# An early decay table, transposes in groups between output tiles, later splits of the output weights and six banks at the end, in a gated linear-attention kernel

## The reference

```
xn   = layernorm(x)
qkv  = silu(xn @ w_qkv.T); 16 heads of 128
for each block of 64 tokens and each head, with s the head's slope:
    out = (q * decay_q) @ kv + ((q @ k.T) * decay) @ v
    kv  = exp(-64 s) * kv + (k * decay_k).T @ v
out  = norm_w * out / rms(out) over all 16 heads
s    = (sigmoid(xn @ w_gate.T) * out) @ w_out.T
f    = xn * sum(top 8 weights) + top 8 weights @ expert_bias   (softmax router, 64 experts)
y    = x + s * silu(f)
```

## Time and profile before

| | |
|---|---|
| median of 3 runs | 1200.68 us (1197.55 to 1203.21) |
| profiled execution, its own time | 1200.99 us |
| its span, first to last instruction | 1199.2 us |
| mean granted clock of PE | 0.973 of full speed |
| PE busy | 1121.5 us (94%) |
| DVE busy | 843.1 us (70%) |
| ACT busy | 611.6 us (51%) |
| POOL busy | 128.2 us (11%) |
| DMA | 85.46 MB, 71 GB/s |

### The profile page before, as it was taken

The page is one execution under the profiler, slowest core; times in us unless marked ns, Lnnn a source line. Parts: engine busy times, 40 slices in busy tenths (PEclk is TensorE's granted clock), DMA queues, the critical chain, the costliest instruction groups (busy, mean ns, idle before and its releaser), DMA issues.

```text
span 1199.2 us, 16261 instructions
## 1 busy us (share of the span) xinstructions
PE 1121.5 (94%) x6366; PEld 968.0 (81%) x6366; DVE 843.1 (70%) x1613; ACT 611.6 (51%) x1308; POOL 128.2 (11%) x123
## 2 busy tenths in 40 slices
PE   6949999999999999999789899999999999999996
PEld 4747988889897888889668679898888888898884
DVE  7447678685777868786654877777668687766655
ACT  4436455464655555464524554655555474645542
POOL 4100000000000010202220000000000000000002
PEclk8979999999999999999889899999999999999998
DMA  3162112121111323322210611111212122111403
GB/s 126 36 192 63 41 53 71 54 78 55 53 41 48 97 71 91 112 62 80 78 55 19 219 64 52 62 51 49 78 50 74 36 71 65 50 54 45 132 1 123
DMA packets 37566, 85.46 MB, mean 71 GB/s; under 512 B 4320, under 2 KB 8688, under 8 KB 37488
## 3 DMA queue, kind: packets, MB, share of 16 engines
q1 hardware_dynamic: 37488, 84.41, 22.0%
HBM read 73.88 MB, written 14.71 MB: 74 GB/s over the span
## 4 chain that ended last, share of the span: by engine, by line
PE 64%; DVE 16%; ACT 13%; DMA 3%; SPq 1%; issue 1%; POOL 1%; DVEq 0%
PE psR L215 40%; PE psB L215 12%; PE psO L215 6%; PE psS L215 5%; ACT sg L513 3%; DVE gl L377 3%; ACT gh L376 2%; ACT zh L709 1%; DVE ql L372 1%; SPq L82 1%; DVE T L704 1%; DVE T L555 1%; DVE xl L298 1%; ACT woh L376 1%; DMA dtab<-dscr 1%
## 5 line engine op out<-in xcount | busy, mean ns | idle before, releaser
L724 POOL TENSOR_TENSOR ss<-ss,sq 128x512 f32<-128x512 f32 x58 | 78.4, 1352 | 840.9 <-ACT sq L710 840.9
L215 PE MATMUL psR<-xh,gh 128*128 128x512 f32 x384 | 130.7, 421 | 4.4 <-DVE gl L377 2.3
L215 PE MATMUL psR<-xl,gh 128*128 128x512 f32 x384 | 120.5, 395 | 0.0
L709 ACT ACTIVATE zh<-T,nw 128x512 fp32r<-128x512 f32 x64 | 46.3, 724 | 143.4 <-DVE T L704 143.4
L215 PE MATMUL psR<-xh,gl 128*128 128x512 f32 x384 | 119.3, 392 | 0.0
L215 PE MATMUL psR<-woh,zh 128*128 128x512 f32 x252 | 106.2, 422 | 1.9 <-DVE yacc L763 1.6
L215 PE MATMUL psB<-xh,gh 128*128 128x512 f32 x288 | 93.1, 404 | 15.0 <-ACT psB L506 8.4
L215 PE MATMUL psR<-woh,zl 128*128 128x512 f32 x252 | 100.1, 397 | 0.0
L215 PE MATMUL psR<-wol,zh 128*128 128x512 f32 x252 | 99.8, 396 | 0.0
L215 PE MATMUL psR<-wvh,xh 128*128 128x256 f32 x512 | 87.2, 293 | 8.4 <-DVE xl L298 5.8
L215 PE MATMUL psB<-xh,gl 128*128 128x512 f32 x288 | 89.7, 393 | 0.0
(11 more groups left out here) (186 smaller groups left out, 2668.9 us busy)
## 6 DMA issues: line engine op xcount, KB each, us to landing
raw<-w SPq DMA_DIRECT2D x80, 512.0 KB, 3.5
D<-dtab SPq DMA_DIRECT2D x32, 256.0 KB, 2.7
xs<-x SPq DMA_DIRECT2D x28, 256.0 KB, 3.2
gscr<-xs SPq DMA_DIRECT2D x16, 256.0 KB, 2.0
xs<-xnorm SPq DMA_DIRECT2D x16, 256.0 KB, 3.4
out_dram<-yacc SPq DMA_DIRECT2D x16, 256.0 KB, 2.2
dtab<-dscr SPq DMA_DIRECT2D x2, 1792.0 KB
xs<-gscr SPq DMA_DIRECT2D x14, 256.0 KB, 4.5
```

The source lines that it names most:

```text
L215: return lambda e: e.matmul(o, l, r, start=start, stop=stop, skip_group_check=shared)
L709: hi = act.do(lambda a: a.activation(zh[:, i, :], T[:, t, :], ACT.Copy, scale=half), z, nw_ev, *zfree)
L724: a = lane.do(lambda g: g.tensor_add(ss[:, j, :], ss[:, j, :], sq[:, :]), q, ss_ev.get(j))
```

## The change

- The power for `dval` is queued ahead of the value weights; its DMAs and the spreading come right behind the normalisations of tiles 4 to 7, before the key weights.
- `value_weights(0)` takes its third step ahead of `stat` of tiles 4 to 7. All four mingles at the start, and those at the change of phase, are on DVE.
- `tile_b` becomes a generator `groups_b`; `second_rows` yields after each group. `closing` alternates these groups with output tiles of pair 6 (`do_out(v - 1, 1)`, moved here from `heads`) and pair 7, with key weights and with the values of the next phase.
- In `opening`, `do_scores(v, 1)` comes earlier, and the value weights of the next pair are taken inside `second_keys`, where `do_state(v, 1)` comes behind p5.
- `gates` hands its output-weight split over to the next `first_keys`, behind p6 and p2.
- `fetch` and `finish_tile` are one tile per hook instead of two.
- In `gated`, `last` settles before the sum of squares. At the end, two tiles are seeded in two banks of `psS` before the others, and `add_out` of tiles 0 and 1 comes before the last mix.

```diff
         def groups_b(t, a, b, nb):
...
+            yield
@@ gated
             owed.append(rest)
+            if last:
+                settle()
@@ leave
-            else:
+            elif i >= 0:
                 ring.give(i, e)
@@ hooks of the second phase
-        for k in range(4):
-            for tt in (2 * k, 2 * k + 1):
-                later(8, k, lambda tt=tt: fetch(tt))
-                later(8, k + 1, lambda tt=tt: finish_tile(tt // 4, tt))
+        for tt in range(8):
+            later(*step((8, 0), tt), lambda tt=tt: fetch(tt))
+            later(*step((8, 0), tt + 1), lambda tt=tt: finish_tile(tt // 4, tt))
@@ start
+        e = pool.do(lambda g: g.tensor_scalar(dexp[:, :], dexp[:, :], sl[:, :], None, ALU.mult), sl_ev, dexp_ev)
+        dval_ev = pool.do(lambda g: g.tensor_tensor(dval[:, :], ebase[:, :], dexp[:, :], ALU.pow), e, ebase_ev)
         vw = value_weights(0)
...
         for t in range(4):
             put(t, 0, turned[t])
+        next(vw)
         for t in range(4, 8):
             stat(t, *rows_of[t])
+        settle()
@@ first_keys
             p6()
+            ow = rest_of_out.pop() if rest_of_out else iter(())
+            next(ow, None)
             p2()
+            next(ow, None)
             p7()
@@ second_keys (early is vw is None)
             if early:
                 do_mix(v, 1)
-            else:
-                do_state(v, 1)
             p5()
             if not early:
+                do_state(v, 1)
+                next(vw)
+            p6()
+            if not early:
+                next(vw)
                 do_mix(v, 1)
-            p6()
             split_values(1, 0)
             p2()
+            if not early:
+                next(vw)
+                settle()
             p7()
@@ gates
-            next(ow)
-            settle()
-            next(ow)
+            rest_of_out.append(ow)
@@ opening
             do_mix(v, 0)
+            do_scores(v, 1)
             split_values(0, 1)
-            vw = value_weights(v + 1)
-            next(vw)
-            do_scores(v, 1)
-            next(vw)
             hook(v, 2)
-            next(vw)
-            second_keys(v, prep(GG, v + 1), False)
+            second_keys(v, prep(GG, v + 1), value_weights(v + 1))
@@ closing (put_on is next(fill); both(f, ...) is f(...), then put_on)
+            heads(v, iter(()), True)
+            hook(v, 4)
             second_keys(v, iter(()))
+            put_on()
             do_scores(v, 2)
             split_keys(1)
             split_queries(1)
+            vw = value_weights(v + 1)
+            next(vw)
+            put_on()
+            ow = out_weights(v)
+            do_out(v - 1, 1, between({}, put_on, both(do_state, v, 2), put_on, lambda: next(vw)))
+            next(ow)
+            next(ow)
             do_mix(v, 2)
             split_values(1, 1)
+            put_on()
             do_scores(v, 3)
+            put_on()
+            do_out(v, 0, between({}, both(do_state, v, 3), last_unit, put_on, lambda: next(vw)))
+            put_on()
+            do_out(v, 1, between({}, put_on, put_on, put_on, put_on))
+            qw = weights(QK0, v + 1)
+            next(qw)
+            half_values(0, 0)
+            put_on()
...
@@ second_rows
+            for t in range(4):
+                (a, lda), (b, ldb) = pairs.pop(t)
+                tile_a(t, a, lda)
+                yield
+                yield from groups_b(t, a, b, ldb)
+                if t < 2:
+                    get(t + 2)
+                if t < 3:
+                    mingle(t + 1)
+                    yield
@@ before opening(0)
         for t in range(4):
             norm[4 + t] = normalise_act(4 + t, *rows_of[4 + t])
+        dscr_ev = (...)
         spread_decay(0, 1)
         load_decay(0)
         load_decay(1)
         spread_decay(1, PAIRS)
+        qw = weights(QK0, 0)
+        next(qw)
+        next(qw)
+        mingle_first(0, dve)
+        settle()
+        mingle_first(1, dve)
+        place_first(0)
+        next(qw)
+        place_first(1)
+        mingle_first(2, dve)
+        settle()
+        next(qw)
+        half_values(1, 0)
+        place_first(2)
+        mingle_first(3, dve)
...
@@ end
         rms(0)
+        for t in range(2):
+            add_out(0, t, 8 + t, four[t], done[t])
         do_mix(v, 3, True)
         done += [part_out(0, t, (1,), four[t]) for t in range(2, 4)]
+        spare = [(psS[:, k * 512:k * 512 + 512], -1, s_free[0]) for k in range(2)]
+        for t in range(2):
+            seed_out(1, t, spare[t])
+            part_out(1, t, (0,), spare[t])
+        for t in range(2, 4):
             add_out(0, t, 8 + t, four[t], done[t])
+        for tt in range(12, 16):
+            fetch_row(tt)
         for t in range(4):
             end_aside(0, t, 8 + t)
+        rms(1)
+        spare += banks()[:2]
+        for t in range(2, 4):
+            seed_out(1, t, spare[t])
+            part_out(1, t, (0,), spare[t])
         for t in range(4):
+            final_tile(1, t, 12 + t, spare[t], part_out(1, t, (1,), spare[t]))
```

More of the change, by code:

```diff
@@ L1119, in between @@
                 yield
+        rest_of_out = []
         def first_keys(v, nx):
@@ L1136, in first_keys, with second_keys @@
             split_queries(0)
-        def second_keys(v, nx, early=True):
+        def second_keys(v, nx, vw=None):
             p1, p5, p6, p2, p7, p3, p4 = seven(QK1, nx)
+            early = vw is None
             p1()
@@ L1231, in closing, with both, last_unit @@
         def closing(v, fill):
-            heads(v, value_weights(v + 1))
+            heads(v, iter(()), True)
+            hook(v, 4)
             second_keys(v, iter(()))
[L1234 to L1237, removed]
+            put_on = lambda: next(fill)
+            def both(fn, *rest):
+                return lambda: (fn(*rest), put_on())
+            def last_unit():
+                do_mix(v, 3)
+                put_on()
+            put_on()
             do_scores(v, 2)
@@ L1240, in closing @@
             split_queries(1)
-            next(fill)
-            do_state(v, 2)
+            vw = value_weights(v + 1)
[5 more added lines that the diff above has]
+            next(ow)
             do_mix(v, 2)
             split_values(1, 1)
+            put_on()
             do_scores(v, 3)
-            next(fill)
-            do_state(v, 3)
-            do_out(v, 0)
-            do_mix(v, 3)
-            next(fill)
-            do_out(v, 1)
-            next(fill)
+            put_on()
[5 more added lines that the diff above has]
+            half_values(0, 0)
+            put_on()
+            next(qw)
+            half_values(0, 1)
+            put_on()
+            next(qw)
+            put_on()
+            next(qw)
+            half_values(1, 0)
+            put_on()
+            next(qw)
+            half_values(1, 1)
+            settle()
         pairs = {}
@@ L1260, in mingle @@
             (a, lda), (b, ldb) = pairs[t]
[L1261 to L1284 removed]
+            combine(t, a, lda, b, ldb, dve)
+        def second_rows():
+            for t in range(4):
+                (a, lda), (b, ldb) = pairs.pop(t)
+                tile_a(t, a, lda)
+                yield
+                yield from groups_b(t, a, b, ldb)
[3 more added lines that the diff above has]
+                    mingle(t + 1)
+                    yield
         def mingle_first(t, lane):
@@ L1323, in build @@
         )
-        half_values(1, 1)
-        split_values(0, 0)
         spread_decay(0, 1)
@@ L1329, in build @@
         spread_decay(1, PAIRS)
+        qw = weights(QK0, 0)
+        next(qw)
+        next(qw)
+        mingle_first(0, dve)
+        settle()
+        mingle_first(1, dve)
+        place_first(0)
+        next(qw)
+        place_first(1)
+        mingle_first(2, dve)
+        settle()
+        next(qw)
+        half_values(1, 0)
+        place_first(2)
+        mingle_first(3, dve)
+        settle()
+        next(qw)
+        place_first(3)
+        settle()
+        half_values(1, 1)
+        split_values(0, 0)
         opening(0)
@@ L1381, in build @@
         rms(0)
+        for t in range(2):
+            add_out(0, t, 8 + t, four[t], done[t])
         do_mix(v, 3, True)
         done += [part_out(0, t, (1,), four[t]) for t in range(2, 4)]
-        for t in range(4):
+        spare = [(psS[:, k * 512:k * 512 + 512], -1, s_free[0]) for k in range(2)]
[3 more added lines that the diff above has]
+        for t in range(2, 4):
             add_out(0, t, 8 + t, four[t], done[t])
+        for tt in range(12, 16):
+            fetch_row(tt)
         for t in range(4):
             end_aside(0, t, 8 + t)
-        for tt in range(12, 16):
-            fetch_row(tt)
-        four = banks()
-        for t in range(4):
-            seed_out(1, t, four[t])
-            part_out(1, t, (0,), four[t])
-            if t == 2:
-                rms(1)
-        for t in range(4):
-            final_tile(1, t, 12 + t, four[t], part_out(1, t, (1,), four[t]))
+        rms(1)
```

(3 more changed lines are left out.)

50 lines of the change are left out of this document (4 added, 46 removed).

## The result

The changed kernel takes 1164.60 us (median of 4 runs, 1163.89 to 1165.87), beside 1199.88 for the kernel before: a ratio of 0.9705, 95% interval 0.968 to 0.9731, so 2.95% faster. The forecast of 1156 is 8.6 us low, and the time lies in the range of 1145 to 1172. The profiled execution took 1164.4 us (span 1162.6 and 1.8 around it), against 1201.0 before: 36.6 us less, where the sum said 45.5 less.

A forecast was written before the change was run, and what follows sets the result against it. PE, busy 1121.5 of 1199.2 us, was taken as the bound, so only idle time and half clock could be won. 1201.0 + 5.7 − 18.4 − 6.0 − 9.8 − 14.0 − 3.0 = 1155.5, so 1156 us; range 1145 to 1172.

The forecast's parts named there:

- Start: Before the first key product: value products held back to 18.8 us, then half clock; costs 5.7 us, bounds +8.5 and +1.
- Opening(0): First opening: early decay table removes waits and half clock, later loads still in time; gains 18.4 us, bounds −19.4 and −6.
- Output weights: Steady pairs: splitting output weights later removes 13 of 14 PE waits for the psB seed; gains 6.0 us.
- Opening(8): Second opening: new order removes the kt wait (6.0), single finished tiles give 1.4 and 3.9, v = 9 costs 1.5; gains 9.8 us.
- Change of phase: Groups alternating with output and value tiles take 64.21 us to about 50, PE still the bound; gains 14 us.
- End: End of kernel: two seeds in psS remove PE's 2.6 us bank wait, final tile starts earlier; gains 3.0 us.
- A: Opening(0): the stall moves to another load, QK1 or value weights; costs 13 us, time 1169; chance 0.10.
- D: Later output-weight split is late for do_out: 14 waits at wol of 1.2 us each, time 1173; chance 0.07.
- E: Change of phase: all 32 bank uses wait for DVE's backlog; gains vanish or the kernel is slower, 1220; chance 0.02.
- F: A part of the change does nothing, leaving the time within 0.5%; chance 0.01.
- B: Change of phase: DVE, at 38 of 44 us, binds it; the stretch gives back 10 us, time 1166; chance 0.12.
- C: Start: value products are not held back, as when DVE catches up; +1 instead of +5.7 us, time 1151; chance 0.08.

The follow-up runs named there:

- value step put back: Changed kernel with the third step of the first value weights behind the normalisations of tiles 4 to 7 again: 1161.52 us, ratio 0.9666.
- start reordered: Changed kernel with third value step and weights' sums behind the first two mingles, the power on POOL behind the four rstd: 1159.58 us, ratio 0.9659.
- table late: Changed kernel with the decay table's power and transfers behind the last mingle of the start again: 1176.08 us, ratio 0.9787.
- table alone: Kernel before, with only the decay table's power and transfers moved early as in the changed kernel: 1185.08 us, ratio 0.9874.
- the run that moves the router's split: Start reordered, plus the router's split one hook earlier and zl's owed halves settled ahead of the transposes: 1158.02 us, ratio 0.9631.

## Why the prediction held, point by point

**Start, +5.7 against +7.1.** Mechanism shown (value step put back, start reordered). Against this one trace the term is 1.4 too small: the last value group, behind two short waits of 1.16 and 0.59 us, took 5.3 us at half clock where the walk gave it 3.0, and the groups ahead of it gave 0.9 back. But in eight kernels with equal code the first key product comes 5.1 to 8.1 us later than in the kernel before, and +5.7 lies within that: the size is neither confirmed nor refuted to better than that.

**Opening(0), −18.4 against −16.3.** Mechanism shown from both sides (table late, table alone). Of the 2 us missing, 1.0 is in the work, 53.3 us of busy PE at clock 0.99 where I had worked out 52.3 by taking half clock out of the earlier trace rows (the run with the table alone has 52.9 at clock 1.00); the other is in the waits, 2.0 us where I left 1.0. All covers stood: PE waits for no weight load, D or kt there. One part of the reasoning was not needed: I had counted the moved value weights among what covers the table, and the run with the table alone, in the old order, takes 55.06 us too. The stuck queue that spoke against the change costs what the late table costs, 12.2 us here.

**Output weights, −6.0 against −5.5.** Shown by its own run at 5.8 in the same two stretches and about 7 in all, with the 13 waits that the forecast had counted, and the fourteenth (v = 1) stayed as it said. Its cause, ACT held by the router's split behind POOL, is shown by the run that moves the router's split, where moving that split takes the wait away.

**Opening(8), −9.8 against −7.0.** Up to scores(8, 3) the gain is 4.3, where I had 7.4, and its cause was not the one that I named. I gave 6.0 to the new order of the opening (kt no longer behind the value split) and 1.4 to the finished tiles. With the order put back the stretch loses 0.4; with two tiles at a hook again it loses 4.0. The step that failed is thus the 6.0 for kt: its wait of 3.3 did go, but with the old order and single tiles it is 1.9 already, and in the new order 1.4 for T and 1.1 for the psB seed stand in its place, beside 1.0 for gl. That the term came out within 3 us is in part luck: the tiles gave what I had credited to the order. The part behind scores(8, 3) was right, −4.2 against −3.9, and the four tiles moved on to v = 9 cost the 1.5 that I charged.

**Change of phase, −14.0 against −11.0.** Shown by undoing it, to some 2 us. The stretch of the earlier trace rows takes 53.14 us where I had 50: 6.5 of idle time, where the walk of the banks gave 5 to 6, and 46.7 of busy PE, where I had 44.0 at full clock. 3.0 of the 46.7 ran at half clock, behind the wait for zl, so 1.5 of the miss is clock, 1.2 is work that I had sized too small, and at most 0.5 is the sum of the waits. The walk came near with that sum, but not with its parts: it had ql (1.3 forecast, 1.42 measured) and the banks (1.9, measured 1.5), but not 3.04 for zl. DVE does zl in order behind an xl, which waits for ACT. I had looked at how long DVE is busy and at who waits for a bank, not at what stands in front of zl. That the wait is not simply an added 3 us is what the run with zl settled earlier shows: with 1.9 of it gone the stretch is as long as before.

**End, −3.0 against −3.9.** Shown by its own run (3.7). Measured from scores(15, 3), the first final tile starts 19.4 us in, against 22.8 before: 3.4 sooner, where I had 2.8. The other 0.5 is a wait of 0.52 us of DVE for a row of x in the kernel before, which the forecast did not have; it went with the earlier `fetch_row`.

**The sum.** All but one of the six terms erred to the side of too much gain or too little cost, and the six together by 8.9 us. The two openings and the change of phase make up 7.9 of it; in each, the trace after has new waits of 1 to 3 us where longer ones were taken away, for which the sum had left a small allowance. The width of the range was given too small from the bounds: half of their widths, combined as squares, come to 10.8 us each way, not to about 9. Rivals A, D, E and F did not happen, B is ruled out by the run with the mingles on POOL, and C is contradicted by the product at 18.70.

## What to carry to other kernels

A list of waits is not a list of gains: behind each wait on an in-order engine stands the next one, so read what is queued second before pricing the first as gone, and leave 1 to 3 us per place. When a change bundles edits, cost the one that moves a long transfer by itself: here it alone was worth 16 of the 35 us, and the reordering of the openings nothing once the table was early. A term that comes out near its forecast is not yet explained: in opening(8) only the runs that undo one edit each showed which of the two had made it. Look for waits of 2 us or more on PE that a short piece of unrelated work causes (here the split of the router's weights, behind POOL): this one cost its length and, in five of nine kernels with equal code, 1.6 us of half clock behind it.

## What was not expected of the hardware

The same wait of 2.24 us with the same instructions around it left the clock at 2.4 GHz in four kernels and brought it to 1.2 in five, a difference of 1.6 us. Such places lie in the start and the change of phase too, where equal code spread over 2.5 and 1.6 us (2.3 in the old code of the change of phase), which is as much as several of the differences that the edits were to show. What decides whether the clock falls is not settled: no run was made for it.
